# Four of eight padding transfers moved ahead of one tile's row load at the seam between the two stages of a Mamba and mixture-of-experts kernel

## The chip, the cores and the metric

The kernel runs on one core of one Trainium2 chip. The metric is device time in microseconds (us) of one execution. The core has five engines that run side by side and meet only at semaphores: TensorE (PE; PEld is its weight load), VectorE (DVE), ScalarE (ACT), GpSimd (POOL) and SyncE (SP). SP computes nothing here: it reads a few numbers into registers and issues most of the DMA transfers. The transfers of all engines run on the same 16 DMA engines of the core.

## The reference, cut to what matters

Input is x, 8 sequences of 512 tokens with 256 features. A Mamba block (projection, short convolution, a scan over 16 states per feature, gate, output projection) with its norm comes first, and then a mixture of 8 experts of which each token uses 4:

```python
x = _layernorm(x + mamba(x))                       # stage 1
logits = x @ router_weight.T + router_bias
topk_logits, topk_idx = jax.lax.top_k(logits, 4)   # 4 of 8 experts for each of the 4096 tokens
topk_w = jax.nn.softmax(topk_logits)
gate, up = jnp.split(einsum('nd,ejd->nej', x, gate_up_proj) + gate_up_proj_bias, 2, axis=-1)
act = (clip(up, -7, 7) + 1) * minimum(gate, 7) * sigmoid(1.702 * minimum(gate, 7))
out = einsum('nei,edi->ned', act, down_proj) + down_proj_bias
x = _layernorm(x + einsum('ned,ne->nd', out, combine))
```

## The kernel before, in words

**Three stages.** Stage 1 does the Mamba block, one sequence a round, and sends every token's row (256 features, its number and its 8 expert weights, 272 floats) to four of eight queues in HBM, the tensor `queues`, one queue for each expert. POOL does this with indirect DMAs. Stage 2 works through tiles of 512 rows, each of one queue, so of one expert. Stage 3 normalizes the sums.

**Tiles of stage 2.** There are 36 tiles or a little more; which expert and which rows a tile has is computed on the chip (`expert_i`, `row_i`). The first six (`EARLY = 6`, tiles 0 to 5) are full tiles that can be known before the last three sequences are routed; they are written out one by one. From tile 6 on a loop runs over pairs of tiles. Buffers alternate with the tile's parity: even tiles use `first_raw` (weights) and `first_rows` (rows), odd tiles `raw_w` and `xq`.

**What a tile needs.** Its weights (`load_weights`, L597, one transfer of 1668 KB) and its rows (`load_rows`, L606, one transfer of 544 KB). TensorE transposes the rows of tile t+1 (`transpose_tile`, L508, eight matmuls) in the middle of tile t, right behind the first chunk of tile t's up projection (L524), and goes on with the down projection of tile t-1 (L1550). Its order is fixed, so it stands still if the rows are not there; before its first transpose it waits for the semaphore of the row load. The results of a tile are added to `total` in HBM by four indirect DMAs of POOL (`add_output`, L1663).

**Padding.** A queue's last tile may be only partly filled. Hence, when all tokens are counted (`base_i`, semaphore `s_ends` at 3), SP writes one block of 512 empty rows (544 KB from the tile `pad`) behind the end of each of the 8 queues. This is `write_ends`, L617 (reads where the queue ends) and L618 (the transfer). Only tiles from 6 on can meet padding. So SP waits for all nine padding transfers (`s_pad` at 16 * (E + 1), L1705; the ninth is the spare block of L611) and for all scattered rows before it loads the rows of tile 6.

**SP's order.** All transfers of SP go through one hardware queue, called q1 in the profile. At tile t SP issues the weights and the rows of tile t+1: the weights when tile t-1's raw weights have been read (`s_wl`, `s_bias`), the rows when tile t-1's rows have been transposed and its token numbers copied (`s_tr`, `s_tok`, `s_share`; the token copy is DVE's L578). At tile 4 this is followed by the eight padding transfers, and then come tile 6's weights and rows. "The rows of tile 5" are the transfer `xq<-queues` that SP issues at tile 4.

The lines around a transfer of rows are:

```python
def load_rows(sp, t):
    row = sp.value_load(row_i[0:1, bass.ds(t.n, 1)], ...)
    after(sp, s_tok, t.n - 1); after(sp, s_share, t.n - 1); after(sp, s_tr, KD * (t.n - 1))
    sp.dma_start(xq[t.p][:, :, :], queues[bass.ds(row, TILE), :]...).then_inc(s_rows[t.p], 16)
```

Of the kernel before, what the change touches and what calls it, by code (L numbers as in the profile page):

```python
# [26 lines left out]
E, TOPK, INNER = 8, 4, 512  # L27
# [78 lines left out]
EARLY, EARLY_SEQS = 6, 5  # L106
# [48 lines left out]
def build(nc, ctx, ins, out):  # L155
    def sem(name):
        return ctx.enter_context(nc.semaphore(name))
# [169 lines left out]
    def after(eng, s, n):  # L327

        if not isinstance(n, int) or n > 0:
            eng.wait_ge(s, n)  # L330
# [79 lines left out]
    s_ends, s_spare = sem("s_ends"), sem("s_spare")  # L410
# [182 lines left out]
    def load_weights(sp, t):  # L593
        expert = sp.value_load(expert_i[0:1, bass.ds(t.n, 1)], min_val=0, max_val=E - 1)
        after(sp, s_wl, 2 * (t.n - 1))
        after(sp, s_bias, t.n - 1)
        sp.dma_start(raw_w[t.p][:, :], ins["w_experts"][bass.ds(expert, 1), :, :].rearrange("e p c -> (e p) c"))\  # L597
          .then_inc(s_w[t.p], 16)


    def load_rows(sp, t):
        row = sp.value_load(row_i[0:1, bass.ds(t.n, 1)], min_val=0, max_val=E * QUEUE)
        after(sp, s_tok, t.n - 1)
        after(sp, s_share, t.n - 1)
        after(sp, s_tr, KD * (t.n - 1))
        sp.dma_start(xq[t.p][:, :, :], queues[bass.ds(row, TILE), :].rearrange("(p a) c -> p a c", a=SUBS))\  # L606
          .then_inc(s_rows[t.p], 16)

    def write_spare_rows(sp):

        sp.dma_start(queues[E * QUEUE:, :].rearrange("(p a) c -> p a c", a=SUBS), pad[:, :, :]).then_inc(s_pad, 16)  # L611
        sp.dma_start(total[TOKENS:, :].rearrange("(p a) d -> p a d", a=SUBS), pad[:, :, 0:D]).then_inc(s_spare, 16)

    def write_ends(sp, some):

        for e in some:
            row = sp.value_load(base_i[0:1, e:e + 1], min_val=e * QUEUE, max_val=e * QUEUE + TOKENS)  # L617
            sp.dma_start(queues[bass.ds(row, TILE), :].rearrange("(p a) c -> p a c", a=SUBS), pad[:, :, :]).then_inc(s_pad, 16)  # L618
# [897 lines left out]
    def tiles(eng, ends):  # L1516

        for k in range(EARLY):
            yield Seq(k // 2, k % 2)
        eng.wait_ge(s_tables, 2)  # L1520
        last_p = last_pair(eng)
        ends.append(last_p)
        with eng.Fori(EARLY // 2, last_p + 1) as pair:
            for k in range(2):
                yield Seq(pair, k)

    def has_earlier(t):

        return not isinstance(t.half, int) or t.n > 0
# [148 lines left out]
    def sp_stage2(sp):  # L1678
        ends = []

        def load(t):
            load_weights(sp, t)
            load_rows(sp, t)

        def scattered(seqs):

            for i in range(2):
                sp.wait_ge(s_scat[i], 16 * TT * TOPK * ((seqs + 1 - i) // 2))

        bank, n = ROUNDS[SEQS - 1].block("in3")  # L1690
        sp.wait_ge(bank_read[bank], n)
        sp.wait_ge(s_tables, 1)
        load_weights(sp, Seq(0, 0))
        scattered(EARLY_SEQS)
        load_rows(sp, Seq(0, 0))
        sp.wait_ge(s_y, SEQS)
        load(Seq(0, 1))
        sp.wait_ge(s_ends, 2)
        write_spare_rows(sp)
        for t in tiles(sp, ends):  # L1700
            if isinstance(t.half, int) and t.n == EARLY - 1:
                sp.wait_ge(s_tables, 2)
                load_weights(sp, t.at(1))
                scattered(SEQS)
                sp.wait_ge(s_pad, 16 * (E + 1))  # L1705
                load_rows(sp, t.at(1))
            elif has_earlier(t):
                load(t.at(1))
            if isinstance(t.half, int) and t.n == 4:
                sp.wait_ge(s_ends, 3)  # L1710
                write_ends(sp, range(E))
        return ends[0]

    stage2_ends = []
# [1 line left out]
    with nc.Block() as block:  # L1716
        @block.tensor
        def _(pe):
            pe_stage1(pe)
            pe_stage2(pe)  # L1720

        @block.scalar
        def _(act):
            act_stage1(act)
            act_stage2(act)

        @block.vector
        def _(dve):
            dve_stage2(dve, dve_stage1(dve))

        @block.gpsimd
        def _(pool):
            pool_stage2(pool, pool_stage1(pool))

        @block.sync
        def _(sp):
            sp_stage1(sp)
            last_p = sp_stage2(sp)
            waits = [(s_w[0], 16 * (last_p + 2)), (s_rows[0], 16 * (last_p + 2))]
            waits += [(s_add[i], ADDS * (last_p + 1)) for i in range(2)]  # L1740
            stage2_ends.extend(waits)
# [110 lines left out]
```

## Time and profile before

| | us |
|---|---|
| median of 3 runs | 1254.55 (1253.52 to 1254.76) |
| the profiled execution, its time | 1253.93 |
| its span, first to last instruction | 1252.1 |
| PE busy | 1144.7 (91%) |
| DVE busy | 1043.4 (83%) |
| ACT busy | 872.8 (70%) |
| POOL busy | 759.1 (61%) |

The profiled execution took 1.8 us more than its span and lies 0.6 us below the median. Stage 2 goes from about 550 us to 1210 us of the span. From there on times "at 642.74" are microseconds from the start of the span. The granted TensorE clock is given as a share of full speed; it has two levels in this profile, 1.00 (2.4 GHz) and 0.50 (1.2 GHz).

### The profile page before, as it was taken

To read this page: it belongs to the slowest core of one execution; us is meant where nothing else is said; L and a number is where in the kernel's file an instruction comes from. 1 tells how busy PE (TensorE), PEld (TensorE's weight loads), DVE (VectorE), ACT (ScalarE), POOL (GpSimd) and SP (SyncE) were. 2 spreads that over 40 slices of the span, in tenths; PEclk is the share of its full clock that TensorE was granted. 3 is DMA by queue.
4 is the path that set the end of the run, shared out by engine and by line. 5 is a ranking of instruction groups with operands and counts; after the bars stand their busy time and mean duration, and the time that the engine had idled before them with its cause. 6 is when DMAs were issued, how large, how long until landed. Compare 5 with 4: busy or idle time off the path is not lost. (4 is left out here: it accounts for less than half of the span.)

```text
span 1252.1 us, 17793 instructions
## 1 busy us (share of the span) xinstructions
PE 1144.7 (91%) x5150; PEld 795.0 (63%) x5150; DVE 1043.4 (83%) x1797; ACT 872.8 (70%) x1553; POOL 759.1 (61%) x535
## 2 busy tenths in 40 slices
PE   9889998999999997688999999999999999999950
PEld 4334353535343443257888888888888888888850
DVE  4999999999999999978876777777777777777744
ACT  4685959595969696625776777677777677677745
POOL 0456659888888887986764544454445544454453
PEclk9899999999999998898999999999999999999985
DMA  2643444646364645555796666656666566665638
GB/s 95 232 171 137 137 180 151 214 162 226 146 231 152 222 166 192 190 194 194 221 296 174 147 170 164 170 133 162 170 159 163 136 172 171 160 143 154 170 40 275
DMA packets 69263, 217.27 MB, mean 174 GB/s; under 512 B 7520, under 2 KB 43232, under 8 KB 56288
## 3 DMA queue, kind: packets, MB, share of 16 engines
q1 hardware_dynamic: 33888, 171.63, 37.4%
q0 software_dynamic: 26880, 36.72, 17.8%
q10 hardware_dynamic: 8448, 8.39, 2.0%
q8 instruction: 18, 0.29, 0.1%
q14 instruction: 29, 0.24, 0.1%
HBM read 165.55 MB, written 51.15 MB: 173 GB/s over the span
## 5 line engine op out<-in xcount | busy, mean ns | idle before, releaser
L1155 DVE TENSOR_TENSOR_SCAN state<-decay,p_bu 128x512 f32<-128x512 f32 x256 | 297.1, 1201 | 1.4 <-ACT decay L897 1.4
L697 PE MATMUL p_y<-read,small 128*128 128x512 f32 x512 | 252.6, 633 | 40.7 <-POOL read L1347 40.6
L1663 POOL DMA_INDIRECT total<-o_v,tok x136 | 252.8, 1859 | 37.5 <-issue 36.9
L697 PEld LDWEIGHTS p_y<-read,small 128*128 128x128 f32 x512 | 100.0, 201 | 178.6 <-issue 108.2
L1661 POOL TENSOR_TENSOR scrap<-neg_half 128x1 f32<-128x1 f32 x36 | 22.8, 633 | 271.6 <-ACT o_v L1579 259.2
L534 ACT ACTIVATE gate_v<-p_g,bias 128x512 f32<-128x512 f32 x144 | 98.7, 686 | 118.4 <-PE p_up L524 114.2
L542 DVE TENSOR_SCALAR up_v<-up_v 128x512 f32<-128x512 f32 x144 | 69.6, 483 | 129.7 <-ACT up_v L537 128.8
L897 ACT ACTIVATE decay<-dt,scan_rate 128x511 f32<-128x511 f32 x256 | 162.3, 709 | 10.6 <-DVE state L1155 10.0
L1347 POOL TENSOR_TENSOR read<-state,bc 128x1024 f32<-128x1024 f32 x64 | 127.6, 2000 | 27.8 <-DVE p_bu L1146 13.5
L555 ACT ACTIVATE ah<-a_v 128x512 fp32r<-128x512 f32 x144 | 91.5, 635 | 58.8 <-DVE a_v L548 58.8
L1389 POOL DMA_INDIRECT queues<-rows,index x112 | 115.5, 1031 | 26.8 <-issue 24.9
L571 DVE TENSOR_TENSOR al<-a_v,ah 128x512 fp32r<-128x512 f32 x144 | 98.6, 685 | 12.2 <-ACT ah L555 12.2
L548 DVE SCALAR_TENSOR_TENSOR a_v<-gate_v,up_v 128x512 f32<-128x512 f32 x144 | 99.8, 693 | 5.0
L537 ACT ACTIVATE up_v<-p_up,bias 128x512 f32<-128x512 f32 x144 | 98.2, 682 | 0.0
L1347 POOL TENSOR_TENSOR read<-state,first_wh 128x1024 f32<-128x1024 f32 x32 | 63.9, 1997 | 54.3 <-DVE p_bu L1146 44.6
L1550 PE MATMUL p_o<-first_wh,ah 128*128 128x256 f32 x288 | 83.5, 290 | 2.3 <-DVE al L571 2.3
L1550 PE MATMUL p_o<-wh,ah 128*128 128x256 f32 x288 | 81.9, 284 | 1.1 <-DVE al L571 1.0
L1550 PE MATMUL p_o<-first_wl,ah 128*128 128x256 f32 x288 | 81.6, 283 | 0.0
L1550 PE MATMUL p_o<-first_wh,al 128*128 128x256 f32 x288 | 81.4, 283 | 0.0
L1146 DVE TENSOR_TENSOR p_bu<-p_u,bc 128x512 f32<-128x512 f32 x128 | 81.2, 680 | 0.0
L1550 PE MATMUL p_o<-wh,al 128*128 128x256 f32 x288 | 80.3, 279 | 0.0
L1550 PE MATMUL p_o<-wl,ah 128*128 128x256 f32 x288 | 80.3, 279 | 0.0
(247 smaller groups left out, 2984.6 us busy)
## 6 DMA issues: line engine op xcount, KB each, us to landing
bc<-bc_rows SPq DMA_DIRECT2D x32, 1024.0 KB, 4.8
first_raw<-in_w_experts SPq DMA_DIRECT2D x19, 1668.0 KB, 7.0
raw_w<-in_w_experts SPq DMA_DIRECT2D x18, 1668.0 KB, 7.1
first_wh<-bc_rows SPq DMA_DIRECT2D x16, 1024.0 KB, 4.7
first_wl<-bc_rows SPq DMA_DIRECT2D x16, 1024.0 KB, 5.0
first_rows<-queues SPq DMA_DIRECT2D x19, 544.0 KB, 3.6
xq<-queues SPq DMA_DIRECT2D x18, 544.0 KB, 3.7
queues<-pad SPq DMA_DIRECT2D x9, 544.0 KB, 6.2
```

The source lines that it names most:

```text
L534: act.activation(gate_v[i % 2][:, :], p_g[i % 2][:, :], ACT.Silu, bias=bias[t.p][:, 0, i:i + 1], scale=ALPHA)
L537: act.activation(up_v[i % 2][:, :], p_up[i % 2][:, :], ACT.Identity, bias=bias[t.p][:, 1, i:i + 1])\
L548: dve.scalar_tensor_tensor(a_v[i % 2][:, :], gate_v[i % 2][:, :], TOP, up_v[i % 2][:, :], ALU.min, ALU.mult)\
L555: act.activation(ah[:, i, :], a_v[i % 2][:, :], ACT.Copy).then_inc(s_ah, 1)
L571: dve.tensor_tensor(al[:, i, :], a_v[i % 2][:, :], ah[:, i, :].bitcast(F32), ALU.subtract).then_inc(s_al, 1)
L697: mm = pe.matmul(p_y[h][:, :], ident[:, :], read[:, t % 4, h, :], start=False, stop=(t == SLOTS - 1))
L897: act.activation(decay[(SLOTS * s.n + t) % AHEAD][:, h, 1:LEN], dt[s.p][:, h, 1:LEN], ACT.Exp, scale=rate[:, h, t:t + 1])\
L1155: dve.tensor_tensor_scan(state[t % 4][:, h, :], decay[(SLOTS * s.n + t) % AHEAD][:, h, :], p_bu[:, h * LEN:(h + 1) * LEN], 0.0, ALU.mult, ...
L1347: pool.tensor_tensor(read[:, t % 4, :, :], state[t % 4][:, :, :], of_state(t, 1), ALU.mult).then_inc(s_read, 1)
L1389: pool.indirect_dma_start(queues, bass.IndirectOffsetOnAxis(ap=index_of(s)[:, i:i + 1], axis=0), rows_of_seq(s)[:, i // TOPK, :], None).th ...
L1550: mm = pe.matmul(to, v[:, i, a * P:(a + 1) * P], w[t.p][:, c:c + D], start=(i == 0 and a % 2 == 0 and m == 0), stop=(i == CH - 1 and m == ...
L1663: pool.indirect_dma_start(total, bass.IndirectOffsetOnAxis(ap=tokens_of(t)[:, a:a + 1], axis=0), output_of(t)[:, a, :], None, compute_op=A ...
```

## The change

At tile 4 (`EARLY - 2`), SP issues the weights of tile 5, then four padding transfers (queues 0 to 3), then the rows of tile 5, then the other four. Before, the eight stood together behind the rows of tile 5. Nothing is added or left out.

```diff
@@ sp_stage2, in the loop over tiles
                 scattered(SEQS)
                 sp.wait_ge(s_pad, 16 * (E + 1))
                 load_rows(sp, t.at(1))
+            elif isinstance(t.half, int) and t.n == EARLY - 2:
+                load_weights(sp, t.at(1))
+                sp.wait_ge(s_ends, 3)
+                write_ends(sp, range(E // 2))
+                load_rows(sp, t.at(1))
+                write_ends(sp, range(E // 2, E))
             elif has_earlier(t):
                 load(t.at(1))
-            if isinstance(t.half, int) and t.n == 4:
-                sp.wait_ge(s_ends, 3)
-                write_ends(sp, range(E))
```

SP before, from the weights of tile 5 (row 118) to the first padding transfer; `raw_w` are the weights, `xq` the rows of tile 5, and seven more padding transfers follow:

```order
117 L597 ISA [waits s_bias,s_wl]
118 L597 DMA raw_w<-in_w_experts 128x3336
119 L602 TENSOR_LOAD row_i
120 L602 ISA x2
121 L606 ISA [waits s_tr,s_share,s_tok]
122 L606 DMA xq<-queues 128x1088
123 L617 TENSOR_LOAD base_i [waits s_ends]
124 L617 ISA x2
125 L618 ISA
126 L618 DMA queues<-pad 128x1088
```

The rows of tile 5 are the first transfer behind the weights there. SP now, from the third of the padding transfers that have moved (row 130; the first stands in row 122, right behind the weights in row 118) to the fifth:

```order
130 L618 DMA queues<-pad 128x1088
131 L617 TENSOR_LOAD base_i
132 L617 ISA x2
133 L618 ISA
134 L618 DMA queues<-pad 128x1088
135 L602 TENSOR_LOAD row_i
136 L602 ISA x2
137 L606 ISA [waits s_tr,s_share,s_tok]
138 L606 DMA xq<-queues 128x1088
139 L617 TENSOR_LOAD base_i
140 L617 ISA x2
141 L618 ISA
```

The rows of tile 5 went from row 122 to row 138, behind four padding transfers in the same queue; the wait for `s_ends` now stands ahead of them too. What follows the eighth padding transfer (weights and rows of tile 6) has kept its place, and no other engine's order has changed.

## Rows read from the trace of the kernel before

**Rows 1.** PE timeline: the transposes of tiles 4 to 7 (start, us, engine, instructions).

```profile
625.24 1.03 PE L508 MATMUL p_x<-small,first_rows 128*128 128x128 f32 x8
...
642.74 1.03 PE L508 MATMUL p_x<-small,xq 128*128 128x128 f32 x8
...
662.73 1.09 PE L508 MATMUL p_x<-small,first_rows 128*128 128x128 f32 x8 [2.20 <-DMA first_rows<-queues]
...
680.29 1.04 PE L508 MATMUL p_x<-small,xq 128*128 128x128 f32 x8
```

**Rows 2.** SP timeline: issues from tile 5's weights to tile 6's rows.

```profile
629.36 0.34 SPq L597 DMA_DIRECT2D raw_w<-in_w_experts  x1
637.35 0.34 SPq L606 DMA_DIRECT2D xq<-queues  x1
638.56 11.90 SPq L618 DMA_DIRECT2D queues<-pad  x8
651.72 0.36 SPq L597 DMA_DIRECT2D first_raw<-in_w_experts  x1
657.21 0.35 SPq L606 DMA_DIRECT2D first_rows<-queues  x1
```

**Rows 3.** SP's waits from 620 to 720 us (waited for: us, times, longest).

```profile
SPq L1705 <- DMA queues<-pad: 4.3, 1, 4.3
```

**Rows 4.** Issue and landing of tile 5's weights, its rows, the last padding.

```profile
L597 SPq DMA_DIRECT2D raw_w<-in_w_experts x1: 338/338/338, 629.4 to 629.4; - x1
...
DMA to landing us min/median/max: 8.3/8.3/8.3
...
L606 SPq DMA_DIRECT2D xq<-queues x1: 338/338/338, 637.4 to 637.4; - x1
...
DMA to landing us min/median/max: 4.1/4.1/4.1
...
L618 SPq DMA_DIRECT2D queues<-pad x1: 332/332/332, 650.1 to 650.1; - x1
...
DMA to landing us min/median/max: 6.2/6.2/6.2
```

**Rows 5.** Issue and landing of tile 1's weights and rows.

```profile
L597 SPq DMA_DIRECT2D raw_w<-in_w_experts x1: 343/343/343, 553.1 to 553.1; - x1
...
DMA to landing us min/median/max: 8.0/8.0/8.0
...
L606 SPq DMA_DIRECT2D xq<-queues x1: 338/338/338, 554.2 to 554.2; - x1
...
DMA to landing us min/median/max: 9.1/9.1/9.1
```

**Rows 6.** Stretches: length, PE, PEld, DVE, ACT, POOL busy, PEclk, DMA share, GB/s.

```profile
639.00:644.00 5.00, 5.00 (x34) 4.41 (x33) 3.12 (x8) 2.77 (x5) 3.26 (x3) 1.00 1.01 394
644.00:657.00 13.00, 13.00 (x78) 11.37 (x77) 10.17 (x16) 10.43 (x20) 5.54 (x5) 1.00 1.06 344
```

**Rows 7.** PE timeline of stage 1: two of the long idle times.

```profile
148.69 9.11 PE L697 MATMUL p_y<-read,small 128*128 128x512 f32 x16 [2.31 <-POOL read L1347]
...
491.45 0.19 PE L739 MATMUL p_bank<-chosen,before 128*128 128x40 bf16 x1 [4.20 <-DVE chosen L1237]
```

**Rows 8.** Stretches behind the idle times that ended at 148.69 and 662.73.

```profile
150.00:153.00 3.00, 3.00 (x5) 1.28 (x4) 2.87 (x4) 3.00 (x7) 2.54 (x2) 0.51 0.83 186
153.00:155.00 2.00, 2.00 (x5) 0.79 (x5) 2.00 (x3) 2.00 (x4) 1.23 (x1) 0.89 0.98 303
...
663.00:680.00 17.00, 17.00 (x103) 15.03 (x102) 11.99 (x22) 10.46 (x18) 5.73 (x4) 1.00 0.59 158
```

**Rows 9.** L1550 alone in two stretches: length, PE and PEld busy, clock, DMA.

```profile
579.00:583.00 4.00, 4.00 (x20) 4.00 (x20) 0.50 0.22 75
620.00:622.00 2.00, 2.00 (x19) 2.00 (x18) 1.00 0.75 199
```

**Rows 10.** DVE timeline: the token copy of tile 4.

```profile
654.92 0.17 DVE L578 CAST tok<-first_rows 128x4 uint32<-128x4 int32 x1 [0.26 <-DMA total<-o_v,tok]
```

## The prediction

> **What bounds the kernel now.** I read the page first (PE is the busiest engine), then stretches around the seam, and there PE is busy throughout: 5.00 of 5.00 us and 13.00 of 13.00 us, at clock 1.00 [rows 6]. So in stage 2 the time is set by PE, and a change to SP's queue counts only where PE waits for a transfer. The PE timeline shows where. The transposes of tile 5 start 17.50 us after those of tile 4, and those of tile 7 start 17.56 us after those of tile 6, but those of tile 6 start 19.99 us after those of tile 5, behind 2.20 us idle that ended with the transfer of tile 6's rows [rows 1]. The seam thus costs 19.99 - 17.50 = 2.5 us over a steady tile, and this is all that better placing of the padding can win.
>
> Why those rows are late is seen on SP. The eight padding transfers are issued from 638.56 for 11.90 us [rows 2], the last lands at 650.1 + 6.2 = 656.3 [rows 4], and SP waited 4.3 us for that at L1705 [rows 3] before it could issue tile 6's rows at 657.21 [rows 2].
>
> The reader should then look at what stands in front of the moved transfers. Tile 5's weights are issued at 629.36 and land at 637.7; tile 5's rows are issued at 637.35 and land at 641.45 [rows 2, 4]. PE takes them at 642.74 without a wait [rows 1]. The cover is 1.3 us.
>
> **The change part by part.** *The later four paddings, and tile 6.* After the change the eight are spread from about 630.6 on. SP needs 1.2 us from a transfer to the first padding behind it (637.35 to 638.56) and 1.65 us from one padding to the next (11.90 less 0.34, by 7) [rows 2]. So the last four, again behind the issue of the rows, run from about 638.6 to 643.5, some 6.6 us before the old end. The last lands near 655 even if the queue stays full, while tile 6's rows wait for the token copy of tile 4, at 654.92 [rows 10] or later. The wait of L1705 goes, the rows of tile 6 are issued right behind that copy as in every steady tile, and PE's 2.5 us there go: **-2.5 us**. What is late next at tile 6 is then nothing: tile 7's rows, in the ordinary pattern, came without a wait [rows 1].
>
> *The issue of tile 5's rows.* The first four paddings are issued at about 630.6, 632.2, 633.9 and 635.5, while SP stood idle before. Reading `row_i` takes it to about 636.7, still ahead of 637.35, which is set by the token copy of tile 3. The issue itself costs **0**; the cover is 0.6 us of SP's idle time.
>
> *The landing of tile 5's rows.* Here is the price. Do transfers of one queue share the engines, or does each follow the one ahead? Tile 1 answers: its rows were issued 1.1 us behind its weights and landed at 554.2 + 9.1 = 563.3, after the weights' 553.1 + 8.0 = 561.1, and not after about 4 us like a transfer on its own [rows 4, 5]. So each follows the one ahead. Tile 5's rows then land five transfers of 544 KB (four paddings and themselves) after the weights' 637.7. What is one worth in a full queue? Eight paddings landed between 641.45 and 656.3: 14.9 / 8 = 1.86 us each, 300 GB/s. The lower bound is the fastest stretch, 394 GB/s with all else in it [rows 6]: 0.557 MB / 394 = 1.41 us. The upper bound is the 2.2 us by which tile 1's rows followed its weights [rows 5]. I take 1.86, since those are the same transfers beside the same output adds of POOL. Landing: 637.7 + 5 x 1.86 = 647.0; bounds 644.8 and 648.7. PE wants the rows at 642.74: **+4.3 us**, bounds 2.1 and 6.0. All of this is on the path, because PE's order is fixed and no work of another kind can step in.
>
> One page gives another rate. The Trainium skill, page "DMA: Bandwidth & Descriptors", section "Specifications", puts the ceiling of the 16 engines at 435 GB/s; five transfers at it would be 6.4 us (an estimate), the stall 1.4 us and the change a gain of 1.1 us. The stretches here stay at 344 and 394 GB/s with the adds in them [rows 6], so I do not go by it.
>
> *The clock.* Between 40 and 665 us the PE timeline has ten idle times of 2.31 us or more, and each has a stretch at half clock that begins within it or right behind it; the five single ones from 1.5 to 2.20 us have none (two shorter ones close together, at 575 us, have one). The shortest of the ten, 2.31 us [rows 7], is followed by 3.4 us at half clock (2 x (3 x 0.49 + 2 x 0.11)); the 2.20 us at tile 6 left the clock at 1.00 [rows 1, 8]. The one nearest in length to mine is 4.20 us [rows 7]. So a stall of 4.3 us should be followed by about 3.4 us at half clock. At half clock the down projection issues 20 matmuls in 4 us, at full clock 19 in 2 [rows 9]: 0.20 against 0.105 us each, so 3.4 us lose 3.4 x (1 - 0.105 / 0.20) = **+1.6 us**. Bounds: 0 (no dip) and 3.2 (a dip twice as long).
>
> *The other engines.* DVE, ACT and POOL fall behind PE by the stall and have slack; all stand in the same fixed order. POOL's adds of tile 1 now share the DMA engines with paddings and may land some us later. They gate POOL's next adds and, through those, the token copy of tile 4, which already waited 0.26 us [rows 10]. With PE 4 us later this is covered: **0**. Without the stall the cover is gone, and each us of delay would count.
>
> **The sum.** -2.5 + 4.3 + 1.6 = +3.4 us. On the profiled execution that is 1253.93 + 3.4 = 1257.3; the median of the runs is 0.6 us above that execution, so 1254.55 + 3.4 = **1257.9 us**.
>
> **The rivals.** *A, a short stall (not slower).* The paddings go through at the lower bound of 1.41 us. Then the rows land at 644.8, PE stands for 2.1 us, below the shortest idle time with a dip, and the sum is -2.5 + 2.1 = -0.4: 1254.2. It decides at about 1.45 us a transfer, where the stall passes 2.3 us. For it: the 394 GB/s at the start of the old paddings. Against it: POOL's adds, which run beside the moved ones. The skill's ceiling above belongs here.
>
> *B, the rows do not queue (not slower).* If a read into the core's memory runs beside writes to HBM, tile 5's rows land in time, and only the gain is left: -2.5, 1252.1. The Trainium skill, same page, section "Two DMAs through the same engine are not ordered", says that transfers in a queue start in order but are pipelined, with separate read and write sides. A start in order still places the rows behind the paddings, and tile 1's rows are a read behind a read, so the trace does not exclude an overlap of a part: each us of overlap takes 1 us off my sum.
>
> *C, a longer delay (slower).* 2.2 us a transfer gives a stall of 6.0, and a dip of 6.8 us costs 3.2: +6.7, 1261.3. Late adds of POOL would land here too.
>
> *D, no difference.* If the paddings' descriptors are taken up so late that rows and paddings cost the same as before, 1254.6. The row order of SP speaks against it.
>
> **How the numbers follow.** The forecast (stall of 3 to 5.5 us with a dip, +2.0 to +5.5) has 0.55; A 0.20, B 0.10, C 0.10, D 0.05. About 0.2% (2.5 us) is what a measurement of this kernel can tell from no change. Of the forecast 0.44 lies above +2.5, with C 0.54 slower. Half of B reaches a gain of 2.5 us and noise adds nothing to speak of: 0.05 faster. The rest, 0.41, is within 0.2%. The range leaves out half of B at the bottom and the upper end of C: 1252.6 to 1261.2. The forecast's own is 1256.5 to 1260.0.
>
> **What the changed profile would show.** Right: PE idle 3 to 5 us ahead of the transposes of tile 5, released by the transfer `xq<-queues`; that transfer 8 to 11 us from issue to landing instead of 4.1; the granted clock at half behind it; no idle ahead of tile 6's transposes and next to no wait at L1705's place. The transposes of tile 7 start near 683.7 instead of 680.29. Wrong: tile 5's rows land within 6 us of their issue (B, or A if at 6 to 7.5), the clock stays at 1.00 behind a stall above 2.5 us, or PE still waits at tile 6.

## The result and the profile after

The changed kernel takes 1256.79 us (median of 7 runs, 1255.31 to 1259.39), the kernel before 1254.76 us in the same comparison (7 runs). The ratio is 1.0026, with a 95% interval of 1.0015 to 1.0037: slower by 0.26%, or 3.3 us of 1254.76. The medians alone differ by 2.0 us and the means by 2.4 us, so the size of the effect is known to about 1 us. The forecast was 1257.9 us, slower by 3.4 us. The profiled execution took 1258.65 us with a span of 1256.8; it lies 1.9 us above the median of its kernel.

The transposes of tiles 4 to 7 after the change, against [rows 1] (PE timeline: start, us, engine, instructions, idle before and releaser):

```profile
625.33 1.03 PE L508 MATMUL p_x<-small,first_rows 128*128 128x128 f32 x8
...
647.29 1.97 PE L508 MATMUL p_x<-small,xq 128*128 128x128 f32 x8 [4.29 <-DMA xq<-queues]
...
667.03 1.04 PE L508 MATMUL p_x<-small,first_rows 128*128 128x128 f32 x8
...
684.53 1.03 PE L508 MATMUL p_x<-small,xq 128*128 128x128 f32 x8
```

The wait moved from tile 6 to tile 5 and grew from 2.20 to 4.29 us. From the transposes of one tile to those of the next it is 21.96, 19.74 and 17.50 us, 59.20 together; before it was 17.50, 19.99 and 17.56, 55.05 together. A steady tile takes 17.50. So tile 5 costs 4.46 us, tile 6 gave back its 2.49 and lost 2.24 again in another way, and tile 7 is 0.06 us shorter: +4.15 us in this pair of traces. (Two single executions: their times lie 4.7 us apart, more than the runs as a whole.)

SP's queue, against [rows 2] (SP timeline):

```profile
629.53 0.34 SPq L597 DMA_DIRECT2D raw_w<-in_w_experts  x1
630.63 4.21 SPq L618 DMA_DIRECT2D queues<-pad  x4
637.45 0.36 SPq L606 DMA_DIRECT2D xq<-queues  x1
638.92 4.31 SPq L618 DMA_DIRECT2D queues<-pad  x4
646.83 0.36 SPq L597 DMA_DIRECT2D first_raw<-in_w_experts  x1
661.57 0.36 SPq L606 DMA_DIRECT2D first_rows<-queues  x1
```

The rows of tile 5 are issued at 637.45, as before. Issue and landing of the weights, of the first and the fourth padding and of the rows, against [rows 4]:

```profile
L597 SPq DMA_DIRECT2D raw_w<-in_w_experts x1: 337/337/337, 629.5 to 629.5; - x1
...
DMA to landing us min/median/max: 8.4/8.4/8.4
...
L618 SPq DMA_DIRECT2D queues<-pad x1: 366/366/366, 630.6 to 630.6; - x1
DMA to landing us min/median/max: 9.4/9.4/9.4
...
L618 SPq DMA_DIRECT2D queues<-pad x1: 336/336/336, 634.5 to 634.5; - x1
DMA to landing us min/median/max: 11.5/11.5/11.5
...
L606 SPq DMA_DIRECT2D xq<-queues x1: 360/360/360, 637.4 to 637.4; - x1
DMA to landing us min/median/max: 9.8/9.8/9.8
```

The weights land at 629.5 + 8.4 = 637.9, the paddings at 640.0, 642.1, 644.1 and 646.0, the rows at 647.2: one behind the other in the order of issue, 9.3 us for five transfers.

The clock behind that wait (a stretch: length, PE, PEld, DVE, ACT, POOL busy, PEclk, DMA share, GB/s), and POOL's and VectorE's side of it:

```profile
644.00:645.00 1.00, 0.00 (x0) 0.00 (x0) 0.59 (x2) 1.00 (x3) 0.00 (x0) 0.99 1.06 374
645.00:652.00 7.00, 4.71 (x22) 4.67 (x23) 2.27 (x3) 1.02 (x2) 5.72 (x4) 0.51 1.05 429
652.00:655.00 3.00, 3.00 (x17) 2.50 (x16) 0.00 (x0) 0.30 (x1) 1.94 (x2) 1.00 1.04 364
```

```profile
645.52 1.20 POOL L1661 TENSOR_TENSOR scrap<-neg_half 128x1 f32<-128x1 f32 x1 [8.07 <-DMA total<-first_o,first_tok]
...
661.24 0.16 DVE L578 CAST tok<-first_rows 128x4 uint32<-128x4 int32 x1
```

From 645 us on the clock is at half for 2 x 7 x 0.49 = 6.9 us; PE stands for the first 2.3 us of them and works in the rest, 4.7 us. POOL waited 8.07 us until its adds of tile 1 had landed. In the kernel before that wait is 2.93 us:

```profile
640.28 0.19 POOL L1661 TENSOR_TENSOR scrap<-neg_half 128x1 f32<-128x1 f32 x1 [2.93 <-DMA total<-first_o,first_tok]
```

### The profile page after: what moved, and what is told of

It reads as the page before. It is cut to its first block and busy times, and to the rows that moved or that the text cites. A ratio compares the mean times of both kernels' runs of the same rounds, so it can differ in the third digit from the quotient of the medians.

```text
span 1256.8 us, 17793 instructions
## 1 busy us (share of the span) xinstructions
PE 1146.8 (91%) x5150; PEld 797.5 (63%) x5150; DVE 1043.6 (83%) x1797; ACT 872.9 (69%) x1553; POOL 759.4 (60%) x535
## 5 line engine op out<-in xcount | busy, mean ns | idle before, releaser
L897 ACT ACTIVATE decay<-dt,scan_rate 128x511 f32<-128x511 f32 x256 | 162.3, 710 | 10.5 <-DVE state L1155 9.9
L571 DVE TENSOR_TENSOR al<-a_v,ah 128x512 fp32r<-128x512 f32 x144 | 98.8, 686 | 12.2 <-ACT ah L555 12.2
L1550 PE MATMUL p_o<-first_wh,ah 128*128 128x256 f32 x288 | 83.5, 290 | 2.3 <-DVE al L571 2.3
L1550 PE MATMUL p_o<-wh,ah 128*128 128x256 f32 x288 | 82.5, 287 | 1.1 <-DVE al L571 1.0
L1550 PE MATMUL p_o<-first_wl,ah 128*128 128x256 f32 x288 | 81.6, 283 | 0.0
L1550 PE MATMUL p_o<-first_wh,al 128*128 128x256 f32 x288 | 81.4, 283 | 0.0
L1550 PE MATMUL p_o<-wh,al 128*128 128x256 f32 x288 | 80.8, 281 | 0.0
L1550 PE MATMUL p_o<-wl,ah 128*128 128x256 f32 x288 | 80.8, 281 | 0.0
```

Source lines behind the costliest of these rows:

```text
L571: dve.tensor_tensor(al[:, i, :], a_v[i % 2][:, :], ah[:, i, :].bitcast(F32), ALU.subtract).then_inc(s_al, 1)
L897: act.activation(decay[(SLOTS * s.n + t) % AHEAD][:, h, 1:LEN], dt[s.p][:, h, 1:LEN], ACT.Exp, scale=rate[:, h, t:t + 1])\
L1550: mm = pe.matmul(to, v[:, i, a * P:(a + 1) * P], w[t.p][:, c:c + D], start=(i == 0 and a % 2 == 0 and m == 0), stop=(i == CH - 1 and m == ...
```

## The experiments

Each ratio is to the kernel before, with its 95% interval. Of each run there is one trace, of one execution. "Seam" is the time from the transposes of tile 4 to those of tile 7; three steady tiles would be 52.5 to 52.7 us.

### The same four paddings, one tile earlier

```diff
-            if isinstance(t.half, int) and t.n == 4:
+            if isinstance(t.half, int) and t.n in (3, 4):
                 sp.wait_ge(s_ends, 3)
-                write_ends(sp, range(E))
+                write_ends(sp, range(4 * (t.n - 3), 4 * (t.n - 2)))
```

> The same four padding transfers as in the change, but issued behind the rows of tile 4 (about 621 us) instead of behind the weights of tile 5; the other four stay behind the rows of tile 5. My theory (only the place in the queue between the weights and the rows of tile 5 costs; spreading them in itself wins the 2.5 us of tile 6): rows of tile 5 land within about 4.5 us of their issue, no PE wait at the transposes of tiles 5 and 6, clock 1.00 through the seam, transposes of tile 7 at 677.8 instead of 680.3, time 2.5 us below the kernel before (ratio about 0.998). Rival (the paddings cost what they cost by their traffic beside POOL's adds, wherever they stand): a new wait elsewhere in tiles 3 to 5 of 2 us or more, ratio 1.000 to 1.003.

Measured: ratio 0.9976 (0.9963 to 0.9989), 3.0 us faster than before, and a seam of 53.34 us, both near what was expected. PE waits at neither transpose. A wait of 0.36 us is seen ahead of tile 5's first chunk, with VectorE's token copy waiting for POOL's adds:

```profile
652.93 0.20 DVE L578 CAST tok<-first_rows 128x4 uint32<-128x4 int32 x1 [0.91 <-DMA total<-o_v,tok]
...
655.50 0.47 PE L524 MATMUL p_g<-xh,wh 128*128 128x512 f32 x1 [0.36 <-issue]
```

So it is not the spreading that costs, but its place: between a tile's weights and its rows. The gain that the forecast took for tile 6 (2.5 us) is real.

### Two ahead

`write_ends(sp, range(2))` ahead of the rows and `range(2, E)` behind them, where the change has four and four.

> Two of the paddings ahead of the rows of tile 5, six behind. The rows should land two transfers of 2.0 us and their own 1.3 to 1.9 us after the weights (637.9): at 643.2 to 643.8. PE waits 0.5 to 1.1 us there, too short for the clock to fall (the longest idle time without a fall was 2.20 us). The last padding lands at about 653.5, so tile 6 doesn't wait. My theory: -2.5 + 0.9 = -1.6 us against the kernel before, ratio 0.9987, clock 1.00. Rival (any padding ahead of the rows costs a stall with a clock dip): ratio above 1.000.

Measured: 1.0029 (1.0016 to 1.0042), as slow as four ahead was in its own comparison, and a seam of 60.89 us. This expectation failed. The wait at the transposes was 1.36 us, not far above the 0.5 to 1.1 us expected, but a larger one followed on the way to tile 5's first chunk:

```profile
642.78 1.09 PE L508 MATMUL p_x<-small,xq 128*128 128x128 f32 x8 [1.36 <-DMA xq<-queues]
...
661.60 0.77 PE L524 MATMUL p_g<-xh,wh 128*128 128x512 f32 x1 [3.78 <-issue]
```

```profile
644.01 1.14 POOL L1661 TENSOR_TENSOR scrap<-neg_half 128x1 f32<-128x1 f32 x1 [8.14 <-DMA total<-first_o,first_tok]
...
659.03 0.20 DVE L578 CAST tok<-first_rows 128x4 uint32<-128x4 int32 x1 [4.33 <-DMA total<-o_v,tok]
```

The trace names no releaser for the 3.78 us, but the chain can be read from it and from the program. POOL's adds of tile 1 land late beside the paddings, so those of tile 2 start at 645.29 (before: 640.62) and land at 659. VectorE's token copy of tile 4 waits for them, and right behind it in VectorE's order stand the remainders of tile 5's weights (L498), without which PE cannot begin: they end at 661.4, PE begins at 661.60. The clock fell to half there as well. Four ahead pays for the rows, two ahead for the adds.

### PE kept busy during the wait

```diff
+        if isinstance(t.half, int) and t.n == EARLY - 1:
+            pe.wait_ge(s_xl, KD * t.n)
+            for j in range(18):
+                pe.matmul(p_x[0][:, :], wh[0][:, 0:P], xh[0][:, 0, :], start=True, stop=True)
         pe.wait_ge(s_rows[t.p], 16 * (t.use + 1))
```

> The changed kernel with 18 more matmuls of 512 columns (into a bank that the transposes then overwrite, their result unused) between the first chunk of tile 4 and the wait for the rows of tile 5: 18 x 0.23 = 4.2 us of PE work in the place of the 4.29 us idle. My theory (the clock is the second half of the loss: 2.24 us between the transposes of tiles 5 and 6 above a steady tile): clock stays at 1.00, transposes of tile 5 start at 647.3 as before the edit or up to 0.3 us later, those of tile 6 17.5 us later, so 2.2 us below the changed kernel: ratio to the kernel before about 1.0015. Rival (the 2.24 us come from operands that other engines deliver late behind the stall): those 2.24 us stay, ratio 1.003.

Measured: 1.0005 (0.9993 to 1.0018), a little below the 1.0015 expected; seam 58.01 us (21.84, 18.68, 17.49). The clock stayed up and the second loss halved, from 2.24 to 1.18 us. PE from 640 to 662 us, and what was left:

```profile
640.00:662.00 22.00, 21.19 (x119) 17.95 (x118) 12.21 (x22) 12.14 (x21) 11.27 (x8) 1.00 0.89 294
```

```profile
657.85 0.20 DVE L582 CAST tok<-first_rows 128x4 uint32<-128x4 int32 x1 [1.35 <-DMA total<-o_v,tok]
...
660.42 0.47 PE L528 MATMUL p_g<-xh,wh 128*128 128x512 f32 x1 [0.81 <-issue]
```

So the half clock made the loss behind the wait. Once it is gone the late adds of POOL show through: VectorE waits 1.35 us for them, and PE 0.81 us of the 1.18 behind that. The theory holds for the clock; that the whole 2.24 us would go was wrong. The changed kernel itself had no wait for the adds there.

### The four paddings on ScalarE's queue

ScalarE reads the four queue ends in tile 2 and issues in tile 3; SP's `write_ends(sp, range(E // 2))` is left out.

```diff
+                if i == 0 and isinstance(t.half, int) and t.n == 3:
+                    for row in ends_at:
+                        act.dma_start(queues[bass.ds(row, TILE), :]..., pad[:, :, :]).then_inc(s_pad, 16)
```

> The four paddings of the change are issued at the same time (about 629.5 us), but by ScalarE through its own queue; SP issues weights and rows of tile 5 right behind each other, then the other four paddings. Same bytes at the same time on the same 16 DMA engines. My theory (the rows wait because they stand behind the paddings in one queue): the weights land later than 637.9, by up to 3 us, but the rows of tile 5 land at 641.5 to 643.5, PE waits 0 to 1 us, no clock dip: 1.5 to 2.5 us below the kernel before, ratio 0.998 to 0.999. Rival (the DMA engines' rate alone decides: the rows cannot be there before all bytes issued earlier have gone): landing at 647, wait 4.3 us, ratio 1.0026.

Measured: 0.9982 (0.9969 to 0.9995). The trace's wait at tile 5 is 1.19 us, the clock stays up, the seam is 54.97 us. It isn't the clean comparison that was meant: ScalarE's queue ran ahead of its arithmetic and issued the four from 623.48 to 625.4, up to 3.4 us ahead of the weights at 626.84, where the change issues them behind. The weights then took 10.9 us to land (8.4 in the change) and the rows 6.5 (9.8). Both readings, the other queue and the head start, explain the shorter wait, and this run doesn't part them.

### Own buffers for tile 4's tokens and output

```diff
+    own_tok, own_o = sb("own_tok", SUBS, dt=U32, at=two), sb("own_o", SUBS, D, at=two)
@@ tokens_of, output_of: tile 4 uses them
@@ copy_tokens
-        if not isinstance(t.half, int) or t.n >= 4:
+        if not isinstance(t.half, int) or t.n > 4:
             dve.wait_ge(s_add[t.p], ADDS * t.use)
```

With two ahead:

> Two paddings ahead as in e2_two_ahead, and tile 4 gets token and output buffers of its own, so that its token copy on VectorE doesn't wait until POOL's output adds of tile 2 have landed (4.33 us in e2_two_ahead). My theory (delayed adds of POOL, through that copy, made the 3.78 us PE wait ahead of the first chunk of tile 5 and the clock dip behind it): the wait of 1.4 us at the transposes of tile 5 stays, the 3.78 us and the dip go, from the transposes of tile 4 to those of tile 7 54 to 54.5 us instead of 60.9, about 1 us below the kernel before, ratio 0.999. Rival (the 3.78 us come from the weights of tile 5, late in another way): they stay, ratio 1.003.

With four ahead and PE kept busy:

> The changed kernel with the 18 extra matmuls of e3_pe_kept_busy and the own buffers of tile 4. My theory (in the changed kernel the loss behind the stall is the clock alone, and in e3_pe_kept_busy the 1.2 us that stayed are VectorE's wait for the adds, uncovered by the clock's return): transposes of tile 6 17.5 us behind those of tile 5, 56.9 us from tile 4 to tile 7 against 58.0 in e3_pe_kept_busy, ratio to the kernel before 1.0015 by this trace sum (e3_pe_kept_busy measured 1.0005, so 0.9995 to 1.0015). Rival: the 1.2 us stay.

Measured: 0.9979 (0.9964 to 0.9994) and 1.0007 (0.9994 to 1.0020). In both traces tile 6 follows tile 5 by 17.65 and 17.64 us, a steady tile. With two ahead the wait at tile 5 was 0.77 us, where 1.4 was expected. But these traces differ from the ones above already ahead of the seam, as the next two runs made clear, so the pair didn't decide by itself.

### Two in each tile, and the changed kernel again

```diff
-            if isinstance(t.half, int) and t.n == 4:
-                sp.wait_ge(s_ends, 3)
-                write_ends(sp, range(E))
+            if isinstance(t.half, int) and 1 <= t.n <= 4:
+                if t.n == 1:
+                    sp.wait_ge(s_ends, 3)
+                write_ends(sp, range(2 * (t.n - 1), 2 * t.n))
```

> The eight paddings in pairs behind the rows of tiles 2, 3, 4 and 5, none ahead of a row load that is near. My theory: no PE wait at the transposes of tiles 5 and 6 and, with only two paddings beside the adds of tile 2, no wait of VectorE for them either (0.91 us in e1_four_one_tile_earlier): 52.7 us from the transposes of tile 4 to those of tile 7, against 53.3 in e1_four_one_tile_earlier and 55.05 before, ratio 0.998. Rival (the first pair stands in the way of the scatters of the last sequence, or SP's wait for the count delays tile 3): new waits in tiles 1 to 3, ratio 0.999 to 1.001.

> The changed kernel once more, unchanged, for the spread of its seam from one execution to another and for its ratio beside the runs above: PE wait of 4 to 4.6 us at the transposes of tile 5, half clock behind it, 59.2 us from the transposes of tile 4 to those of tile 7 within 0.7 us, ratio 1.0026 within 0.001. Rival (the first trace was an outlier): 57 us or less.

Measured: two in each tile 0.9982 (0.9966 to 0.9999) with a seam of 52.63 us, all that can be had. The changed kernel 1.0001 (0.9988 to 1.0014), no longer slower, and a seam of 56.78 us; 1.0026 and 59.2 us were expected, so this expectation failed. Its trace has a shorter wait at tile 5 and a half-clock stretch of 2 x 5 x 0.34 = 3.4 us instead of 6.9:

```profile
653.58 1.09 PE L508 MATMUL p_x<-small,xq 128*128 128x128 f32 x8 [2.41 <-DMA xq<-queues]
...
654.00:659.00 5.00, 5.00 (x26) 4.57 (x24) 1.45 (x2) 0.38 (x1) 1.96 (x2) 0.66 1.10 334
```

Why? Between the transposes of tiles 2 and 3 PE takes 33.1 us instead of 21.2, ahead of anything that the change touches, and POOL isn't late by as much. POOL's adds of tile 1 start at 632.30, the weights of tile 5 only at 637.54; in the traces on which the forecast rests both start at 629.4. Three of the four adds landed at 636.0, 637.9 and 640.7, at most 2.1 us behind the issue of the first padding (638.64); only the fourth was held back, to 647.9.

The lost time between tiles 2 and 3 isn't PE's alone. In this trace PE stands 5.26 us ahead of 593.24, VectorE 2.98 us ahead of 593.01 and ScalarE 5.79 us ahead of 591.72, all marked "issue", with no releaser named, and the granted clock is 0.62 on average from 588 to 606 us (1.00 in the first trace of the changed kernel):

```profile
591.72 0.69 ACT L534 ACTIVATE gate_v<-p_g,bias 128x512 f32<-128x512 f32 x1 [5.79 <-issue]
...
593.01 0.43 DVE L542 TENSOR_SCALAR up_v<-up_v 128x512 f32<-128x512 f32 x1 [2.98 <-issue]
...
588.00:606.00 18.00, 9.75 (x27) 6.69 (x28) 5.62 (x17) 4.90 (x9) 10.03 (x11) 0.62 0.51 180
```

### The kernel before in the other phase, and the pair of two-ahead kernels

> The kernel before itself, for its seam beside the three runs below. In the first pair of traces POOL's adds of tile 1 began at the same time as the weights of tile 5 (629.4 and 629.36 us); in the runs f1 to f4 they began 5 to 8 us ahead of them. I expect the PE wait of 2.2 us (2 to 2.6) at the transposes of tile 6 whatever that phase is, 19.9 to 20.1 us between the transposes of tiles 5 and 6, and ratio 1.000. If the phase mattered here too, the wait would be 1 us or less where the adds come earlier.

> The changed kernel a third time. My theory now: the stall at the transposes of tile 5 depends on when POOL's adds of tile 1 run. Beside the weights and paddings (start within 1 us of the weights): 4.3 us, ratio 1.0026. Started 5 us or more earlier: 2.4 us and a shorter half-clock stretch (3.4 us), ratio 1.000 to 1.001. Rival (the difference between the two measurements was scatter of the runs): the same stall in both phases.

> Two ahead as in e2_two_ahead, for comparison with the next run in one and the same phase. Adds beside the weights: wait of VectorE for the adds of tile 2 of 4 us at tile 4's token copy, PE wait 3.8 us and half clock ahead of tile 5, ratio 1.003. Adds earlier: no such wait, ratio 0.998 to 0.999.

> Two ahead with own buffers for tile 4, in the same phase as the run above. My theory: no PE wait ahead of the first chunk of tile 5 in either phase, ratio 0.998 to 0.999. If the run above shows its 3.8 us wait and this one doesn't, that wait came by tile 4's token copy; if both show none, the pair doesn't decide.

Measured: before against itself 1.0005 (0.9975 to 1.0034); changed 0.9991 (0.9970 to 1.0013); two ahead 1.0002 (0.9980 to 1.0025), above the 0.998 to 0.999 expected; two ahead with own buffers 0.9969 (0.9948 to 0.9989). All four traces have the adds early, as in the changed kernel's second trace; this is called the second phase from here on, and adds that start with the weights the first. The changed kernel's wait of 1.86 us is shorter than the 2.4 expected of it. The kernel before is not the same in it, against the expectation of 2.0 to 2.6 us. Tile 6's rows were issued 28.2 us behind tile 5's weights instead of 27.9, and PE's wait for them ended 6.5 us behind that issue instead of 5.5. The only half clock of its seam stands behind this wait:

```profile
670.51 1.97 PE L508 MATMUL p_x<-small,first_rows 128*128 128x128 f32 x8 [3.46 <-DMA first_rows<-queues]
...
670.00:673.00 3.00, 2.48 (x12) 2.49 (x13) 1.37 (x2) 0.29 (x1) 1.04 (x1) 0.50 0.83 108
673.00:675.00 2.00, 2.00 (x14) 1.87 (x14) 0.00 (x0) 0.00 (x0) 0.00 (x0) 0.89 1.03 406
```

All traces side by side. The number in the column "phase" is the start of POOL's adds of tile 1 less the issue of tile 5's weights; a wait is the idle time ahead of the transposes.

| kernel | phase | wait at tile 5 | wait at tile 6 (in brackets: at the first chunk of tile 5) | tile 4 to 7 | ratio |
|---|---|---|---|---|---|
| before | 0.0 | 0 | 2.20 | 55.05 | |
| changed | 0.0 | 4.29 | 0 | 59.20 | 1.0026 |
| four one tile earlier | 0.0 | 0 | 0 (0.36) | 53.34 | 0.9976 |
| two ahead | 0.0 | 1.36 | 0 (3.78) | 60.89 | 1.0029 |
| PE kept busy | 0.0 | covered | 0 (0.81) | 58.01 | 1.0005 |
| ScalarE's queue | 0.0 | 1.19 | 0 (0.74) | 54.97 | 0.9982 |
| before | -6.1 | 0 | 3.46 | 57.60 | 1.0005 |
| changed | -5.2 | 2.41 | 0 | 56.78 | 1.0001 |
| changed | -7.4 | 1.86 | 0 | 56.24 | 0.9991 |
| two ahead | -7.4 | 0 | 0 | 52.84 | 1.0002 |
| two ahead, own buffers | -7.4 | 0.77 | 0 | 53.58 | 0.9979 |
| two ahead, own buffers | -5.5 | 0.26 | 0 | 53.05 | 0.9969 |
| PE busy, own buffers | -7.4 | covered | 0 | 56.83 | 1.0007 |
| two in each tile | -5.7 | 0 | 0 | 52.63 | 0.9982 |

In the first phase the change costs 4.15 us by its traces; in the second it gains 0.8 to 1.4 us.

Three things limit what the table can say. First, the phases come with the chips: the runs of the comparison with the first phase were on chip 6 (that of the first pair isn't recorded), those with the second on chips 3 and 10, where the kernel before takes 1263.30 and 1261.11 us instead of 1254.67. Phase and chip can't be told apart, and no run moved POOL's adds alone. That the phase makes the shorter wait is thus argued from the traces, not shown. Second, seams and ratios agree only to some 2 us: in the four runs on chip 6 the ratio lies 1.3 to 2.3 us below what the seams give against 55.05 (ScalarE's queue has the seam of the kernel before and a ratio of 0.9982).

Third, a trace shows one execution, and the executions of one comparison may be mixed. The runs beside the traces of the second phase have medians of 1259.65 to 1263.65 us, but the 35 runs of the kernel before in the last comparison go from 1254.76 to 1267.98. That may also be why two ahead has a good trace in the second phase and a ratio of 1.0002. The own buffers take 0.0033 off that ratio in the same comparison (0.9969 against 1.0002; 2.05 us between the medians), which fits the adds as the cause in the executions that have the first phase. Neither of the two traces shows the wait ahead of the first chunk, so the pair doesn't decide. With intervals of 0.002 on each side and no trace of both in the first phase it is likely, not shown.

## Why the prediction was right, point by point

**The gain at tile 6, -2.5 us: right.** The 2.20 us wait is gone, and four paddings one tile earlier show that gain alone (-1.7 us by the traces, -3.0 by the runs). One remark beside it was wrong: SP's wait at L1705 did not go but grew, since SP gets there earlier:

```profile
SPq L1705 <- DMA queues<-pad: 6.4, 1, 6.4
```

It ended near 653.6 with the last padding (forecast: near 655), and tile 6's rows were then held by the token copy at 661.24, as the forecast had it. An idle SP costs nothing there.

**The issue of tile 5's rows, 0: right.** 637.45 against 637.35.

**The landing, +4.3 us: right.** Five transfers in 9.3 us at 1.86 each had been taken, five in 9.3 us were measured; PE waited 4.29 us. The mechanism is as forecast: four paddings and then the rows land in the order of issue. (That it is the one queue, and not the traffic on the engines alone, rests on this order; the run on ScalarE's queue doesn't part the two.) That the size agrees to a tenth is partly luck. The single gaps are 2.1, 2.1, 2.0, 1.9 and 1.2 us. And the mean of 1.86 had mixed two kinds: in the kernel before, the first three paddings land at 642.9, 644.3 and 645.8, 1.4 to 1.5 us apart, and the other five take 10.5 us, 2.1 each. What differs is the share of the DMA engines' time that POOL's queue q0 takes beside SP's q1. Its packets, MB and share are, in the kernel before from 639 to 644 and from 644 to 652 us, and in the changed one from 638 to 645.5:

```profile
q0 software_dynamic: 37, 0.03, 3.9%
...
q0 software_dynamic: 523, 0.49, 41.9%
...
q0 software_dynamic: 462, 0.41, 34.1%
```

Four paddings at 2.1 and the rows at 1.45 would have been 9.85 us. Rival B (rows that don't queue) fell: the quicker rows need no overlap, since 0.557 MB at the 427 GB/s of 646 to 647 us are 1.3 us. Rival A fell: the 429 GB/s of the stretch behind 645 us came only when the adds of tile 1 were over, and the 435 GB/s of the Trainium skill (page "DMA: Bandwidth & Descriptors", section "Specifications") were no measure for a queue that shares its engines with adds of 1 KB rows. From 648.5 to 652 us, without a packet of q0, the trace comes to 434. Rival D fell, since the wait moved. Of C the stall of 6.0 us did not come, but the length of its half clock did.

**The clock, +1.6 us: right in kind, too small in size.** The half-clock stretch lasted 6.9 us and not 3.4, the length that stood as the upper bound (3.2 us of cost). It began within the wait, at 645; PE worked 4.7 us of it, and 4.7 x (1 - 0.105 / 0.20) is the 2.24 us that tile 6 lost. The run with PE kept busy took the half clock away.

**The other engines, 0: right for this kernel, and for a reason that was named, but it was the narrowest place.** The forecast said that late adds of POOL are covered as long as PE is 4 us late. POOL could go on with the next adds 5.2 us later (645.52 against 640.28), and this stayed covered: the last add of tile 2 landed at 660.2, 1.0 us ahead of the token copy at 661.24. With two paddings ahead the cover is gone, and the adds cost more (3.78 us of waiting) than the rows do there (1.36). The expectation for that run left them out and missed by 5.3 us.

**The sum.** +3.4 us was forecast, the traces give +4.15 (-2.49, +4.46, +2.24 and -0.06), the runs +3.3 (interval 1.9 to 4.6). The transposes of tile 7 start at 684.53, where 683.7 was forecast. With runs that scatter by 4 us, the agreement of 3.4 with 3.3 says less than the three terms do.

**What the forecast did not see** is that all of this holds in the traces of one phase only. It took the profile of before as the only timing. In the other comparisons the changed kernel is at 1.0001 and 0.9991, neither slower nor faster. There PE loses time between the transposes of tiles 2 and 3, together with ScalarE and VectorE, and three or all four adds are over when the paddings come. For PE's idle time ahead of 593 to 595 us some traces name no releaser (5.26 us, "issue") and some VectorE (3.21 and 2.55 us, `al`, L571 of the kernel before). The cause of that lost time stays open; it wasn't tried.

## What to carry to other kernels

Behind a large transfer in the same queue, every transfer put ahead of an urgent small one delays that one by its full service time (1.9 to 2.1 us for each of the four here): look for the cover of what is overtaken (1.3 us here) before the gain of what overtakes. Bulk without a deadline belongs behind the most urgent load of a tile and a tile or two early, in small lots: four one tile earlier (0.9976), two in each tile (0.9982) and two ahead with own buffers (0.9979 and 0.9969) were all faster than the kernel before, with intervals below 1, and the changed kernel in no comparison was. And bulk transfers delay not only their own queue: what other queues have in flight, and who waits for that, belongs in the sum, as does a second look at whether the timing before is the only one.

## What the runs showed of the hardware that was not expected

**Adds of another queue are held back too.** POOL's four adds of tile 1 take 4.9 to 7.5 us from issue to landing in the kernel before and 9.6 to 10.0 us with four paddings beside them; in the second trace of the changed kernel the first two, over at 637.9 just as the weights were issued, took 3.7 us each. The paddings cost the adds up to 5.1 us more, nearly as much as the 5.7 us of the rows behind the paddings. The last of the four adds, before and after:

```profile
L1663 POOL DMA_INDIRECT total<-first_o,first_tok x1: 2068/2068/2068, 635.3 to 635.3; - x1
DMA to landing us min/median/max: 4.9/4.9/4.9
```

```profile
L1663 POOL DMA_INDIRECT total<-first_o,first_tok x1: 1995/1995/1995, 635.5 to 635.5; - x1
DMA to landing us min/median/max: 10.0/10.0/10.0
```

They land at 639.3, 641.3, 643.4 and 645.5, each 0.5 to 0.8 us ahead of a padding (640.0, 642.1, 644.1, 646.0). The Trainium skill, page "DMA: Bandwidth & Descriptors", section "Queues, rings and completion order", says that an engine takes turns between queues packet by packet and that a semaphore's increment lands only after all earlier writes of that engine, across its queues. The pairs of landings agree with that; no run here parts it from plain sharing of bandwidth.

**A queue of ScalarE runs ahead of its arithmetic.** The first of the four paddings on it was issued at 623.48, 1.9 us before the weight copy that stands ahead of it in ScalarE's order had finished (625.39).

**The half clock outlasts the wait, and not always by the same.** After waits of 2.41, 1.86 and 3.46 us ahead of transposes it lasted 3.4 us, after the 4.29 us 6.9, and in the trace with three engines idle between tiles 2 and 3 it came to 2 x 18 x 0.38 = 13.7 us from 588 to 606. A wait of 1.86 us was followed by one, where in the trace of before waits up to 2.20 us had none: so these traces give no length of wait that is safe.
